# Writing out the context part of a cross-attention kernel, with twelve context tiles in flight and the value means folded into the projection

## What is computed

```
x = x + xattn(layernorm(x), ctx_1024, Wq, Wk, Wv, Wo)   # out.mean over the 4 query groups, @ Wo
x = x + ffn(layernorm(x), weight, bias)                 # sign weights, int8-like input
# in xattn:
kh = einsum('bse,ehd->bshd', ctx, Wk); kh = rope(kh)
vh = einsum('bse,ehd->bshd', ctx, Wv)
scores = einsum('bghsd,bhad->bhsa', qh, kh); attn = softmax(scores / HEAD_DIM**0.5)
```

## Time and profile before

| | us |
|---|---|
| median of 3 runs | 1320.23 (1318.98 to 1321.29) |
| the profiled execution, its own time | 1319.5 |
| its span in the profile | 1317.7 |
| first / last `ctx_kv` starts | 10.12 / 111.91 |
| first scores start | 124.79 |
| PE busy over the span | 1267.9 (96%) |

### The profile page before, as it was taken

The page is one execution under the profiler, slowest core; times in us unless marked ns, Lnnn a source line. Parts: engine busy times, 40 slices in busy tenths (PEclk is TensorE's granted clock), DMA queues, the critical chain, the costliest instruction groups (busy, mean ns, idle before and its releaser), DMA issues.

```text
span 1317.7 us, 36811 instructions
## 1 busy us (share of the span) xinstructions
PE 1267.9 (96%) x9848; PEld 1085.9 (82%) x9911; DVE 1181.8 (90%) x2772; ACT 1025.1 (78%) x2338; POOL 791.2 (60%) x1536
## 2 busy tenths in 40 slices
PE   5897999999999999999999999999969999999998
PEld 5796999999999999999999999999935555555554
DVE  4876899999999999999999999999978888888887
ACT  3454788888888888888888888888857878888886
POOL 3564888888888888888888888888820000000000
PEclk9999999999999999999999999999979999999999
DMA  8574355555555555555546452323108999999945
GB/s 266 166 216 133 107 158 182 154 183 161 176 165 171 165 171 167 170 171 166 178 159 187 150 169 76 102 80 98 37 5 332 400 401 395 401 399 404 406 201 223
DMA packets 100815, 265.18 MB, mean 201 GB/s; under 512 B 49705, under 2 KB 65769, under 8 KB 72114
## 3 DMA queue, kind: packets, MB, share of 16 engines
q1 hardware_dynamic: 100786, 264.86, 58.8%
HBM read 139.64 MB, written 125.17 MB: 201 GB/s over the span
## 4 chain that ended last, share of the span: by engine, by line
DVE 47%; PE 31%; issue 15%; DMA 2%; DVEq 2%; SPq 1%; ACT 1%; POOL 1%; POOLq 0%; ACTq 0%
PE bank L1248 18%; DVE amax L898 10%; DVE x_sb L930 8%; DVE e_sb L944 6%; DVE mx_sb L940 5%; DVE bn_sb L889 5%; PE bank L1239 4%; PE bank L1246 3%; DVE qT_sb L912 2%; PE bank L1065 2%; DVE rinv_sb L886 2%; DVE ve_sb L918 2%; DVE bn_sb L881 2%; DVE mv_sb L904 1%; DMA x_sb<-in_ctx 1%
## 5 line engine op out<-in xcount | busy, mean ns | idle before, releaser
L1248 PE MATMUL bank<-wT,x_sb 128*128 128x512 f16 x1024 | 263.9, 380 | 3.5 <-issue 0.2
L1168 PE MATMUL bank<-wqs,xT_sb 128*128 128x128 f32 x2048 | 259.7, 280 | 0.2
L718 ACT ACTIVATE x_sb<-bank,mean,cols 128x512 f32<-128x512 f32 x256 | 196.0, 774 | 67.6 <-PE bank L1248 67.3
L1168 PEld LDWEIGHTS bank<-wqs,xT_sb 128*128 128x128 f32 x2048 | 238.2, 191 | 7.1 <-ACT xT_sb L640 0.8
L1216 PE MATMUL bank<-v_blk,pT_sb 103*128 103x136 f32 x1536 | 199.0, 279 | 0.3 <-ACT pT_sb L682 0.3
L1216 PEld LDWEIGHTS bank<-v_blk,pT_sb 103*128 103x128 f32 x1536 | 190.6, 190 | 0.5 <-ACT pT_sb L682 0.5
L1248 PEld LDWEIGHTS bank<-wT,x_sb 128*128 128x128 f16 x1024 | 100.5, 98 | 106.8 <-issue 1.6
L930 DVE SCALAR_TENSOR_TENSOR x_sb<-x_sb,negm,bank 128x512 f32 (+1 forms) x256 | 179.5, 742 | 7.9 <-PE bank L1179 2.7
L898 DVE TENSOR_REDUCE amax<-x_sb (+1 forms) x128 | 156.0, 1218 | 23.2 <-DVE bn_sb L889 8.0
L691 ACT ACTIVATE sq_sb<-x_sb 128x512 bf16 (+1 forms) x256 | 161.4, 631 | 18.7 <-DVE x_sb L930 1.4
L1005 DVE TENSOR_TENSOR x_sb<-x_sb 128x512 f32 (+1 forms) x256 | 164.5, 683 | 1.2 <-ACT x_sb L718 1.2
(11 more groups left out here) (126 smaller groups left out, 2584.4 us busy)
## 6 DMA issues: line engine op xcount, KB each, us to landing
out_y<-x_sb SPq DMA_DIRECT2D x112, 1024.0 KB, 7.2
x_sb<-in_x SPq DMA_DIRECT2D x64, 1024.0 KB, 6.5
x_sb<-out_y SPq DMA_DIRECT2D x48, 1024.0 KB, 9.0
x_sb<-in_ctx SPq DMA_DIRECT2D x38, 256.0 KB, 2.8
k_blk<-k_scr SPq DMA_DIRECT2D x256, 19.2 KB, 5.5
k_scr<-x_sb SPq DMA_DIRECT2D x38, 128.0 KB, 2.3
v_scr<-x_sb SPq DMA_DIRECT2D x38, 68.0 KB, 2.3
v_blk<-v_scr SPq DMA_DIRECT2D x128, 10.2 KB
```

The source lines that it names most:

```text
L718: act.activation(u_sb[:, t, :], bank[4 + t][:, :], ACT.Identity, bias=stat_of(mean1, j, t, back), scale=cols[:, 6:7]).then_inc(scaled_t, 1)
L1168: last = pe.matmul(bank[2][:, t * HD:(t + 1) * HD], xT_sb[:, t, c, :], wqs[:, c, :], start=c == 0, stop=c == EC - 1)
L1248: last = pe.matmul(bank[4 + t][:, :], q16T_sb[:, t, c, :], wT[:, c, :], start=False, stop=c == EC - 1)
```

## The change

- The loops over context tiles are written out on all five engines.
- `ctx_sb` has 12 slots (CRING) instead of 4; the first 12 tiles are loaded at the start.
- Only the first 8 columns of the rope tables are loaded first, the rest after tile 5. Wo is loaded by DMAs that ACT issues. Wq and the FFN weight are loaded in four pieces each, one per tile, after tiles 1 to 4 and 6 to 9.
- x of batches 0 to 3 is loaded after the stores of turns 28, 32, 35 and 38 (before: one after turn 3, two among the last turns, the fourth in the attention part).
- `kv_step(0)` and `kv_step(1)` are issued in turns 20 and 24 of SP.
- The value means are four more columns of the projection (WC = 260 instead of 256). For that DVE makes Wv times `wbar`, reduced over 32, in the start; L776 and L781 of every tile are gone.
- The weight preparation of DVE is cut smaller and placed by constants (WQ_SUM, FW_SUM, ...).

```diff
+KFIRST = 8
+CRING = 12
+WC = 2 * HD + HEADS
+WQ_SUM, WQ_MEAN, WQ_CENTRE = 9, 14, 16
+FW_SUM, FW_MEAN, FW_CUT, FW_TERN = 13, 19, 21, 22
+BIAS_ROWS = 17
+FW_T = FW_TERN + 4
+KV_AHEAD = (20, 24)
+X_AHEAD = (28, 32, 35, 38)
...
@@ sync
+            for j in range(CT + 3):
+                if j + CRING <= CT:
+                    rows = P if j + CRING < CT else CLAST
+                    sp.wait_ge(cT_done, j + 1)
+                    sp.dma_start(ctx_sb[0:rows, j % CRING, :], ctx_rows[(j + CRING) * P:(j + CRING) * P + rows, :])\
+                      .then_inc(c_in[j % CRING], 16)
+                if 2 <= j:
+                    rows = P if j - 2 < CT else CLAST
+                    sp.wait_ge(klo_ready, j - 1)
+                    sp.dma_start(k_scr[:, :, (j - 2) * P:(j - 2) * P + rows], kT_sb[:, j % 2, :, 0:rows])\
+                      .then_inc(k_out[j % 2], 16)
+                if j <= CT:
+                    rows = P if j < CT else CLAST
+                    sp.wait_ge(v_copied, j + 1)
+                    sp.dma_start(v_scr[j * P:j * P + rows, :, :], v_sb[0:rows, j % 4, :, :])\
+                      .then_inc(v_out[j % 4], 16)
+
+                if 1 <= j < 1 + EC:
+                    sp.dma_start(wq_sb[:, j - 1, :, :, :].rearrange("p h g d -> p (h g d)"), wq_rows[:, j - 1, :])\
+                      .then_inc(wq_in, 16)
+                elif 6 <= j < 6 + EC:
+                    sp.dma_start(fw_sb[:, j - 6, :], fw_rows[:, j - 6, :]).then_inc(fw_in, 16)
...
+                elif j in X_AHEAD:
+                    x_load(X_AHEAD.index(j))
+                elif j in KV_AHEAD:
+                    b = KV_AHEAD.index(j)
+                    for m in range(2):
+                        sp.wait_ge(k_out[m], 16)
+                        sp.wait_ge(v_out[m], 16)
+                    kv_step(b, b)
...
@@ scalar
+            for n in range(4):
+                act.dma_start(wo4[D * n:D * n + D, :], wo).then_inc(wo_in, 16)
             act.wait_ge(wkv_in, 32)
-            act.activation(wkv_r[:, 0, :, :], wkv.rearrange("p c a n -> p c (a n)"), ACT.Copy).then_inc(whi_ready, 1)
+            act.activation(wkv_r[:, 0, :, 0:HD], wkv[:, :, 0, :], ACT.Copy).then_inc(whi_ready, 1)
+            act.activation(wv_part(0), wv_raw, ACT.Copy).then_inc(whi_ready, 1)
...
@@ vector
-            low_ctx(0, 0)
-            low_ctx(1, 1)
...
+            dve.wait_ge(fsum_done, 1)
+            then(dve.tensor_copy(wbar[:, :], bank[6][:, 0:D]))
+            then(dve.tensor_tensor(wvw, wv_raw, wbar[:, :].unsqueeze(1).unsqueeze(1).broadcast_to([P, EC, HEADS, D]),
+                                   ALU.mult))
+            then(dve.tensor_reduce(wvb, wvw, AX.X, ALU.add))
+            then(dve.tensor_copy(wv_mean(0), wvb))
+            dve.tensor_tensor(wv_mean(1), wvb, wv_mean(0).bitcast(F32), ALU.subtract).then_inc(wvb_ready, 1)
+            low_ctx(0, 0)
+            low_ctx(1, 1)
...
-                dve.wait_ge(v_copied, j + 1)
-                dve.tensor_tensor(vw_sb[0:rows, n % 2, :, :], v_sb[0:rows, n, :, 0:D],
-                                  wbar[0:rows, :].unsqueeze(1).broadcast_to([rows, HEADS, D]),
-                                  ALU.mult).then_inc(kv_read, 1)
...
-                dve.tensor_reduce(v_sb[0:rows, n, :, D:D + 1].rearrange("p h a -> p (h a)"),
-                                  vw_sb[0:rows, n % 2, :, :], AX.X, ALU.add).then_inc(v_ready, 1)
...
@@ tensor
-                        last = pe.matmul(bank[2 + m][0:rows, 0:2 * HD], cT_r[m][:, a, c, 0:rows], wkv_r[:, b, c, :],
+                        last = pe.matmul(bank[2 + m][0:rows, 0:WC], cT_r[m][:, a, c, 0:rows], wkv_r[:, b, c, :],
```

More of the change, by code:

```diff
@@ L206, in build @@
         fpos = early(EC, E)
+        fsum4 = early(EC)
         w16 = early(EC, E // 2).bitcast(F16)
@@ L334, in _ @@
-            sp.wait_ge(zeroed, ZEROED)
[L335 to L350, removed]
@@ new lines, in x_load, with kv_step @@
+            def x_load(b):
+                sp.dma_start(x_sb[:, b, :, :], xv[b]).then_inc(x_in[b], 16)
+            def kv_step(b, k):
+                at_least(sp, sc_done_t, 4 * (b - 2) + 4)
+                for h in range(HEADS):
+                    sp.dma_start(k_blk[D * h:D * h + D, k % 2, :, CTX * h:CTX * h + CTX],
+                                 k_scr[D * h:D * h + D, :, bass.ds(b * CTX, CTX)]).then_inc(k_in[k % 2], 16)
+                at_least(sp, pv_done, 2 * (b - 2) + 2)
+                for c, r, n, h, a in SEGS:
+                    sp.dma_start(v_blk[r:r + n, k % 2, c, h, :], v_scr[bass.ds(b * CTX + a, n), h, :])\
+                      .then_inc(v_in[k % 2], 16)
@@ L394, in store_x1 @@
                   .then_inc(x1_out[k], 16)
[L396 to L410, removed]
             kv_step(2, 2)
@@ L488, in _ @@
             pool.wait_ge(ktable_in, 32)
[L489 to L494, removed]
+            for j in range(CT + 1):
+                if j == KFIRST:
+                    pool.wait_ge(krest_in, 32)
                 ctx_step(j, j % 2, P if j < CT else CLAST)
@@ L597, in _ @@
             ctx_step(0, 0)
[L598 to L602, removed]
-            with act.Fori(1, CTAIL // 4) as g:
-                for n in range(4):
-                    ctx_step(g * 4 + 1 + n, (n + 1) % 2)
-                    ctx_late(g * 4 + n, n, g)
-                    keys_out(g * 4 + n - 2, n % 2, g * 2 + n // 2 - 1)
-            for j in range(CTAIL, CT + 3):
+            for j in range(CT + 3):
                 if j + 1 <= CT:
@@ L828, in _ @@
                     then(dve.tensor_tensor(fbias, fbias, bpart16, ALU.subtract))
-                    then(dve.scalar_tensor_tensor(out=brow[0:BR, :], in0=fbias, scalar=rcol[:, 5:6], in1=brow[0:BR, :],
-                                                  op0=ALU.mult, op1=ALU.add))
-                elif j == 13:
-                    then(dve.tensor_copy(ident16[:, :], ident[:, :]))
-            with dve.Fori(CHEAD // 4, CTAIL // 4) as g:
-                for n in range(4):
-                    low_ctx(g * 4 + n + 1, (n + 1) % 2)
-                    ctx_step(g * 4 + n, n, g)
-                    low_keys(g * 4 + n - 2, n % 2)
@@ L838, in _ @@
-            for j in range(CTAIL, CT + 3):
-                if j < CT:
-                    low_ctx(j + 1, (j + 1) % 2, P if j + 1 < CT else CLAST)
-                if j <= CT:
-                    ctx_step(j, j % 4, j // 4, P if j < CT else CLAST)
-                if j - 2 < CT:
-                    low_keys(j - 2, j % 2)
-                o = j - CTAIL
-                if o == 0:
+                    then(dve.scalar_tensor_tensor(out=brow[0:BR, :], in0=fbias, scalar=rcol[:, 5:6],
+                                                  in1=brow[0:BR, :], op0=ALU.mult, op1=ALU.add))
```

232 lines of the change are left out of this document (107 added, 125 removed).

## The result

| | before | after |
|---|---|---|
| median of 12 runs, us | 1320.2 (1317.74 to 1322.82) | 1322.39 (1321.09 to 1325.97) |
| the profiled execution, its own time | 1319.5 | 1321.29 |
| its span | 1317.7 | 1318.4 |
| first `ctx_kv` / tile 1 / tile 9 | 10.12 / 14.28 / 39.70 | 12.04 / 15.46 / 33.95 |
| tile 24 / tile 38 | 76.59 / 111.91 | 70.99 / 112.51 |

The account below looks back on a forecast made before the run. PE, 96% busy, was taken as the bound, so only an earlier start of attention counts. Tile 38 was to come 6.5 us earlier and first scores to win 0.8 more: 1320.2 - 7.3 = 1312.9 us, range 1305 to 1320.

Parts of the forecast that it names:

- the landing of the key stores: Context tiles: a key store takes 2.3 us to land and has 3.3, so 1.0 us of backlog is free.
- the clock: Rival, behind the `kv_step` stalls: PE's clock falls, two times 1.9 us, 1316.7; chance 0.24 together with written-out code.
- all DMA doubt of tiles 1 to 9: Tiles 1 to 9: weight quarters raise DMA to 2.2 to 2.5 us a tile; 1.2 us lost, ends 0 and 3.
- The early `kv_step`s: Turns 20 and 24: ten issues delay the key store behind them; 2.4 and 3.5 us lost, together 5.9.
- x loads: Three megabyte loads ahead of key stores in the context part hold them back; 0.3 us each, 0.9 lost.
- First scores: Start of attention: PE no longer waits 1.78 us for keys, but q comes late, so 0.8 us is won.
- The start: Up to tile 1: `ctx_kv(0)` waits for value-mean columns, 13.0 against 10.12, 2.9 us later; tile 1 at 16.6.
- The ring: Tiles 1 to 9: twelve context slots end the waits for context rows; eight tiles at 2.0 are 16.0 us.
- DVE's pieces: Tiles 9 to 24: weight preparation beyond 0.46 us delays `ctx_kv` two tiles on; 34.8 us instead of 30.
- ternary chunks: Tiles 24 to 38: each of four chunks costs 0.5 us, 2.0 in all.
- written-out code: Rival, context loops: instruction loading costs up to 0.2 us a tile, 4.8 back, 1317.7; chance 0.24 together with the clock.
- SP as the bound: Rival, context part: issues of 0.8 us make every key store late, 1329; chance 0.14, including other waits as dear.

Follow-up runs that it names:

- b: The changed kernel with four key slots instead of two; 1310.42 us, ratio 0.9919 to the kernel before.
- l: The changed kernel with the value stores issued by ACT instead of SP, nothing else; 1318.79 us, ratio 0.9989 to the kernel before.
- c: The changed kernel with four key slots and the two early `kv_step`s issued behind all stores; 1309.58 us, ratio 0.9923 to the kernel before.
- d: The changed kernel with 4 context slots instead of 12, the rest of the rope tables loaded after tile 3; 1330.29 us, ratio 1.0078.
- f: The changed kernel with four key slots, eight value slots, and the early `kv_step`s' 20 DMAs one per turn in turns 12 to 31; 1308.54 us, ratio 0.9918.
- i: As f, with x of batches 0 to 3 in sixteen pieces of 256 KB, one per turn from turn 25; 1308.28 us, ratio 0.992.
- k: As i, with the value stores issued by ACT in its pause, one turn later; 1301.46 us (4 runs), ratio 0.9857 to the kernel before.
- j: The changed kernel with only x of batches 0 to 3 cut into sixteen pieces of 256 KB; 1321.22 us, ratio 1.0015.
- e: The changed kernel with x of batches 1, 2 and 3 loaded after turns 38, 39 and 40; 1317.2 us, ratio 0.9984.

## Why the prediction was wrong

In sum it was 9.5 us off: 7.7 at the first scores (125.16 against 117.5), 0.3 more by the end of the span, 1.1 around the span (the profiled execution took 2.9 us more than its span, before 1.8), 0.4 between profiled time and median. The last two are unexplained; the difference of time and span was 1.8 to 2.9 us over all kernels. The 7.7 splits by stretches of `ctx_kv` starts:

| stretch | predicted | after | off by |
|---|---|---|---|
| to tile 1 | 16.6 | 15.46 | -1.1 |
| tile 1 to 9 | 17.2 | 18.49 | +1.3 |
| tile 9 to 24 | 34.8 | 37.04 | +2.2 |
| tile 24 to 38 | 36.8 | 41.52 | +4.7 |
| tile 38 to first scores | 12.1 | 12.65 | +0.6 |

- **The step that failed** is the landing of the key stores; the clock, put at nothing, is the second, below. I took 2.3 us for every tile, the median of before, and counted the 1.0 us of slack that two slots leave as enough; all DMA doubt of tiles 1 to 9 was 1.2 us, and tiles 9 to 24 had none. In the changed kernel a key store took 3.8 us from 20 to 45 us, and 3.3 from its keys being ready was the most it could take. b shows the price: with two more slots tiles 1 to 9 took 16.5 and 9 to 24 35.2, the latter 0.4 from my sum. That is 2.0 and 1.8 us less than with two, against 3.5 that my sum is short by up to tile 24. Over the whole kernel two slots cost 12.0 us, the waits behind the `kv_step`s included.
- *Landing or late issue?* Store by store, of the 7.8 us that ACT waited ahead of tile 13, about 3.2 are late issue, an estimate from SP's and DVE's timelines (SP came to the seven stores 0.03 to 1.09 us after their keys were ready) and the rest is landing, 3.5 to 4.4 us each. In l, ahead of tile 13, the issue was late by more than 0.2 us for one store only, and the longest wait was all landing.
- *Why the landing got longer* is open. A fuller DMA does not explain it by itself: from 62 to 92 us in the kernel before, PE was busy 28.98 of 30 us, the queue 75.6%, and 14 key stores took 2.3 us in the median; from 45 to 62 in the changed kernel the queue was 72.2% busy and they took 3.0. What differs is also the order on SP. Before, a context load stood 1.2 us ahead of the key store, with the value store between; where SP is late in the changed kernel it stands 0.5 us ahead (before, then after):

```profile
64.07 0.37 SPq L324 DMA_DIRECT2D x_sb<-in_ctx  x1
64.70 0.36 SPq L330 DMA_DIRECT2D v_scr<-x_sb  x1
65.25 0.58 SPq L331 DMA_DIRECT2D k_scr<-x_sb  x1
```

```profile
47.82 0.47 SPq L368 DMA_DIRECT2D x_sb<-in_ctx  x1
48.33 0.56 SPq L373 DMA_DIRECT2D k_scr<-x_sb  x1
```

  From 88 us on, where no context rows are left to load, six key stores of the changed kernel with no x load close ahead landed in 2.1 us. No run changed the order alone, so this is a rival, not shown.
- *The early `kv_step`s* went as the prediction had it. ACT's waits were 2.94 and 3.57 us for predicted 2.4 and 3.5, at the places named, and tiles 25 and 29 each started 2.9 and 3.4 us late.
- *The clock* I had only as a rival, at 1.9 us a stall. It fell behind all three waits of PE between tile 24 and 38. From tile 25 to 27 it took 5.8 us (75.84 to 81.65), and the same from tile 29 to 31, where c, without the stalls, took 4.5: 1.3 each. From tile 37 to 38 it took 2.2 instead of c's 1.6. Together 3.3, the largest part of the 4.7. The 1.9 a stall of the rival was too much, the nothing of the sum too little.
- *x loads*: three times 0.3 was too little for one of them. The load at 101.60 stood ahead of the key store at 102.60, that took 5.5 us to land, and tile 37 came 2.0 late. Over the 0.9 that I had for all three this is 1.0. With 0.4 for the `kv_step`s, 3.3 for the clock, 0.3 at tile 31 that I can't place, and the other tiles 0.2 shorter than counted (c), it makes the 4.7, but for rounding.
- *First scores*: the 0.8 us didn't come. The last key copy waited 2.56 us for its slot, at 120.28, and the copy of q for the next steps stood behind it on ACT.
- *The start* was 1.1 us better than I counted. The chain of `wbar` and the product was there, but the transposes of tile 1 ran at 7.36 instead of 8.59, and the matmul with ones_sb at 8.40 instead of about 9.7.
- *The ring* was given the end of the waits for context rows in tiles 1 to 9. d shows that four slots do as well there; the 8 us of the ring lie behind the bursts on SP.
- *DVE's pieces, ternary chunks, written-out code* were right in size. In f tiles 1 to 9 took 15.9 for 16.0, 9 to 24 35.2 for 34.8, in c 24 to 38 29.8 for 30.0. No cost of written-out code can be seen in them.
- *SP as the bound* I gave 1 in 7, with issues of 0.65 us as the point. They took 0.55 in the mean up to 62 us, so it didn't come as described. Near it lies what decides between i and k: with the 0.6 us of a value store off SP's queue, the first scores came 4.1 us earlier and the median fell by 6.8 (the profiled execution of i was 1.4 us below its median). The Trainium skill, DMA: Bandwidth & Descriptors, section Issuing engines are not separate DMA queues, has it that issuing from another engine saves only the time to issue, usually small relative to the DMA itself. Both agree with the traces: the landings got no shorter (3.6 us median in i, 3.7 in k), and an issue is 0.6 us beside them. It was worth several us here because SP had no slack.

So the change took waits away as meant, and gave the gain back in a buffer that it left at its old size, and in the clock behind the waits there.

## What to carry to other kernels

A buffer that was large enough in a kernel with waits need not be so once the waits are gone: when a stage is made faster, set each store's time to land, in the order and at the load that the faster stage will have, against the number of slots times the new pace. Give the other buffers of the pipeline the same depth in the same change; here two more key slots turned a loss of 2 us into a gain of 10, while they brought about one us by themselves. Then count the issuing engine's time per tile like a compute engine's, and let an engine that has a pause take some of the issues. Cutting or spreading bursts moved the waits (f, i, j) but won nothing sure here. And where a stall of the engine that must stay busy is in the sum, its clock behind the stall belongs there too.

## What the runs showed of the hardware

- The landing of a 128 KB store depended much on what else was queued: median 2.3 us before, 3.8 in the changed kernel and 4.4 in b between 20 and 45 us, 2.1 in six stores of the changed kernel from 88 us on, 5.5 behind a megabyte load in the changed kernel and 8.36 in f.
- A single issue on SP can take several times its usual 0.45 to 0.6 us: 1.75 at 76.69 in the changed kernel, with the DMA engines 87% busy, and 2.24 at 26.01 in l, where the next key store was issued 1.37 us after its keys were ready.
- PE's clock fell behind waits of 2.63, 3.23 and 1.74 us; `ctx_kv` then took up to 2.55 us instead of 1.67, until about 5 us after the end of the first two waits. The length of the wait alone doesn't decide it: in e PE stood 2.70 us ahead of tile 25, and its granted clock was 1.00 behind it (`ctx_kv` 1.70 us), while behind 2.06 us in l it was 0.60.
